# A sliding-window attention block inside a fused layer: 32 packed keys per query, values kept stationary in four column groups of TensorE, and the result regrouped by DMA

## The reference

```python
# attention block: 16 heads of 8, 4 key/value heads, window of 32 keys
h = layernorm(xn) ; q, k = rope(h @ Wq + bq), rope(h @ Wk + bk) ; v = h @ Wv + bv
valid = (col <= row) & (row - col < 32)
attn = softmax(where(valid, q @ k.T / sqrt(8), -1e9))
x1 = xn + (attn @ v) @ Wo + bo
y = x1 + gelu(layernorm2(x1) @ Wf1 + bf1) @ Wf2 + bf2      # hidden width 512
# experts: 8 of them, two per token; hidden width 448
z = sum over the token's two experts of g * (silu(xn @ w1.T) * (xn @ w3.T)) @ w2.T
```

## Time and profile before

| what | value |
|---|---|
| median of 3 runs | 540.97 us |
| profiled execution: its own time, its span | 541.51 us, 539.6 us |
| TensorE (PE) busy, share of the span | 461.3 us, 85% |
| VectorE (DVE) | 380.3 us, 70% |
| ScalarE (ACT) | 232.4 us, 43% |
| GpSimd (POOL) | 252.5 us, 47% |
| chain that ended last | PE 57%, DVE 22%, issue 11%, ACT 8% |
| largest lines of the chain | L1112 13%, L1074 11%, L1125 9%, L1053 6% |
| mean granted clock of TensorE | 0.913 of full speed |

### The profile page before, as it was taken

How to read it: one execution, slowest core, us unless ns; L and a number is a source line. 1 busy time by engine, 2 the same in 40 slices (tenths; PEclk the granted TensorE clock), 3 DMA queues, 4 the chain that set the end, 5 groups by cost and what they waited for, 6 DMA issues and landing times.

```text
span 539.6 us, 11287 instructions
## 1 busy us (share of the span) xinstructions
PE 461.3 (85%) x3102; PEld 408.8 (76%) x3103; DVE 380.3 (70%) x1132; ACT 232.4 (43%) x487; POOL 252.5 (47%) x373
## 2 busy tenths in 40 slices
PE   3921687898778999999999999999999998999967
PEld 2810476686668898888888998998988996675657
DVE  6868989779975847758578477584784753447784
ACT  2692433233251454445524544545335455454310
POOL 4626776744650734636437346363462425412520
PEclk9975777768777999999999999999999999999979
DMA  8961411100111455545544555454544540403042
GB/s 220 326 259 35 157 49 41 35 26 30 36 30 44 139 167 144 155 143 140 163 141 132 162 150 155 138 160 148 152 152 136 171 134 7 151 1 97 22 117 79
DMA packets 40571, 63.96 MB, mean 119 GB/s; under 512 B 6718, under 2 KB 27074, under 8 KB 40400
## 3 DMA queue, kind: packets, MB, share of 16 engines
q1 hardware_dynamic: 35456, 54.65, 33.3%
q0 software_dynamic: 4352, 8.47, 4.8%
q10 hardware_dynamic: 720, 0.30, 0.3%
HBM read 48.05 MB, written 15.87 MB: 118 GB/s over the span
## 4 chain that ended last, share of the span: by engine, by line
PE 57%; DVE 22%; issue 11%; ACT 8%; POOL 1%; DMA 1%; DVEq 0%; ACTq 0%; POOLq 0%
PE bank L1112 13%; PE bank L1074 11%; PE bank L1125 9%; PE bank L1053 6%; PE bank L1150 5%; PE bank L1139 4%; DVE rmax L650 3%; DVE pT L667 3%; DVE S L657 2%; PE bank L1086 2%; ACT L906 2%; DVE x_sb L740 2%; PE bank L1048 1%; DVE h L702 1%; ACT act L915 1%
## 5 line engine op out<-in xcount | busy, mean ns | idle before, releaser
L1112 PE MATMUL bank<-xsT,w_sb 128*128 128x128 f32 x1008 | 128.2, 279 | 4.4 <-DVE inter L730 2.7
L1112 PEld LDWEIGHTS bank<-xsT,w_sb 128*128 128x128 f32 x1008 | 119.5, 194 | 7.6 <-issue 5.4
L431 POOL DMA_INDIRECT scratch_ys<-ysb,pair x72 | 71.8, 997 | 36.1 <-issue 24.8
L1074 PEld LDWEIGHTS bank<-vbd,pT 128*128 128x128 f32 x512 | 73.7, 225 | 13.2 <-DVE pT L667 6.9
L1125 PE MATMUL bank<-w_sb,inter 128*128 x576 | 80.2, 282 | 4.1 <-issue 2.0
L1074 PE MATMUL bank<-vbd,pT 128*128 128x36 f32 x512 | 74.6, 303 | 10.3 <-DVE pT L667 9.2
L1125 PEld LDWEIGHTS bank<-w_sb,inter 128*128 128x128 f32 x576 | 71.8, 192 | 8.5 <-issue 7.0
L421 POOL DMA_INDIRECT scratch_xs<-xn_sb,slot x64 | 63.2, 988 | 31.5 <-issue 17.9
L243 POOL TENSOR_TENSOR spare_sb<-eps_sb 128x1 f32<-128x1 f32 x87 | 16.7, 192 | 128.0 <-ACT ysb L921 127.7
L1053 PE MATMUL bank<-kT,qbd 128*128 128x256 f32 x256 | 72.5, 410 | 0.0
L921 ACT ACTIVATE ysb<-bank 128x128 f32<-128x128 f32 x72 | 19.8, 275 | 114.8 <-PE bank L1125 114.8
(11 more groups left out here) (136 smaller groups left out, 692.9 us busy)
## 6 DMA issues: line engine op xcount, KB each, us to landing
w_sb<-in_w SPq DMA_DIRECT2D x72, 448.0 KB, 3.3
scratch_xs<-blank_sb SPq DMA_DIRECT2D x9, 520.0 KB, 6.0
xsb<-scratch_xs SPq DMA_DIRECT2D x72, 65.0 KB, 1.8
w_sb<-scratch_ys SPq DMA_DIRECT2D x8, 512.0 KB, 5.2
w_sb<-in_w SPq DMA_DIRECT2D x1, 2048.0 KB, 10.9
out_dram<-x_sb SPq DMA_DIRECT2D x8, 256.0 KB, 2.3
scratch_ys<-ysb,pair POOLq DMA_INDIRECT x72, 2.6
scratch_xs<-xn_sb,slot POOLq DMA_INDIRECT x64, 2.3
```

The source lines that it names most:

```text
L431: nc.gpsimd.indirect_dma_start(ys, bass.IndirectOffsetOnAxis(ap=pair[:, i % 3:i % 3 + 1], axis=0), ysb[:, i % 3, :], None, bounds_check=2 ...
L1074: last = nc.tensor.matmul(turn_bank[:, n * VW:(n + 1) * VW], pT[:, 2 * n + i].rearrange("p g q -> p (g q)"), vbd[:, p, n + i, :], start=(i ...
L1112: last = nc.tensor.matmul(to[:, c % EC * P:(c % EC + 1) * P], w13_sb[:, i % 3, c * P:(c + 1) * P], xsT[:, p, :], start=True, stop=True)
```

## The change

The diff, cut to its core. Loads and constants follow suit: `older_sb` is a 128 x 32 integer mask of "this place is taken by the older key", `newer_sb` is its complement, `neg_sb` a constant for the first block, which has no block before it; the sums' columns of the values are gone, `vmask_sb` (128 x 32) serves as the weights of the sums.

```diff
 # TensorE
-            def scores(b, p, u): ...          # mask product, two products of 256 columns; 4 calls a batch
+            def own_scores(b, p, h):
+                if some(2 * b + h):
+                    pe.wait_ge(own_kept, 2 * b + h)
+                for i in range(HALF):
+                    n = HALF * h + i
+                    last = nc.tensor.matmul(bank[0][:, i * GW:(i + 1) * GW], qbd[:, p, n].rearrange("p h q -> p (h q)"),
+                                            kT[:, p, :, (n + 1) * WIN:(n + 2) * WIN], start=True, stop=True)
+                last.then_inc(own_psum, 1)
+            def older_scores(b, p, h):
+                if some(2 * b + h):
+                    pe.wait_ge(chosen, 2 * b + h)
...
+                        last = nc.tensor.matmul(bank[1][:, i * GW:(i + 1) * GW], qbd[:, p, n].rearrange("p h q -> p (h q)"),
+                                                kT[:, p, :, n * WIN:(n + 1) * WIN], start=True, stop=True)
             def attend(b, p, quarter, h2T_out):
-                for n in range(quarter * NBLK // 4, (quarter + 1) * NBLK // 4):
-                    for i in range(2):
-                        last = nc.tensor.matmul(turn_bank[:, n * VW:(n + 1) * VW],
-                                                pT[:, 2 * n + i].rearrange("p g q -> p (g q)"),
-                                                vbd[:, p, n + i, :], start=(i == 0), stop=(i == 1))
+                a, total = quarter // 2, quarter % 2
+                for i in range(1 if total else 2):
+                    for c in range(4):
+                        n = 4 * a + c
+                        to = turn_bank[32 * c:32 * c + 32, total * T + a * P:total * T + (a + 1) * P]
+                        weights = (pO if i else pT)[:, n].rearrange("p g q -> p (g q)")
+                        values = vmask_sb if total else dv[:, p, n, :] if i else vbd[:, p, n, :]
+                        last = nc.tensor.matmul(to, values, weights, start=(i == 0), stop=(i == 1 or total == 1))
             def project(b, vt_out):
-                pe.wait_ge(outT_ready, b + 1)
+                pe.wait_ge(outT_in, 16 * 16 * (b + 1))
 # TensorE, step: scores(k, p, 0), (.., 1), (.., 2), (.., 3)  ->  own(.., 0), older(.., 0), own(.., 1), older(.., 1)
 # ScalarE
+            def keep_own(b, h):
+                act.wait_ge(own_psum, 2 * b + h + 1)
+                nc.scalar.activation(S[:, h], bank[0], ACT.Copy).then_inc(own_kept, 1)
 # VectorE
+            def shift(b, h):
+                dve.wait_ge(own_kept, 2 * b + h + 1)
+                wait_apart_dve("older_psum", older_psum, 2 * b + h + 1)
+                nc.vector.copy_predicated(half, bc(older_sb...), bank[1]...).then_inc(chosen, 1)
+                dve.wait_ge(chosen, 2 * b + h + 1)
+                nc.vector.tensor_reduce(rmax[:, h], half, AX.X, ALU.max).then_inc(rowmax_ready, 1)
+                dve.wait_ge(rowmax_ready, 2 * b + h + 1)
+                nc.vector.tensor_tensor(half, half, bc(rmax...), ALU.subtract).then_inc(shifted, 1)
             def norm(b):
-                nc.vector.reciprocal(rsum, pv[:, :, NKV * HD:VW]).then_inc(rsum_ready, 1)     # 128 x 32
+                nc.vector.reciprocal(rsum, turn_bank[:, T:2 * T]).then_inc(rsum_ready, 1)     # 128 x 256
-                nc.vector.transpose(outT, on).then_inc(outT_ready, 1)
+                nc.vector.tensor_tensor(on, turn_bank[:, 0:T], rsum, ALU.mult).then_inc(pv_normed, 1)
 # VectorE, step: the four shifts (2 x 128 x 256 each) and four transposes become two shifts (128 x 512) and two transposes,
 # both transposes at the start of the step
 # VectorE in steps 0 to 6, POOL from step 7 on: pO = pT where the key is of the own block, else 0 (128 x 1024)
+        def newer_part(ops, eng, b): ...
 # POOL: differences of neighbouring blocks of values (128 x 256)
+            def value_steps(b, p):
+                nc.gpsimd.tensor_tensor(dv[:, p], vbd[:, p, 1:NBLK + 1, :], vbd[:, p, 0:NBLK, :], ALU.subtract).then_inc(dv_ready, 1)
 # SyncE
+            def regroup(b):
+                sp.wait_ge(pv_normed, b + 1)
+                for c in range(4):
+                    src = on[c * 32:(c + 1) * 32, :].rearrange("c (a g q) -> c g a q", a=2, g=G)
+                    for g in range(G):
+                        dst = outT[g * 32:(g + 1) * 32, :].rearrange("c (a n q) -> c a n q", a=2, n=4)
+                        sp.dma_start(dst[:, :, c, :], src[:, g]).then_inc(outT_in, 16)
+            for b in range(LEAD - 1):
+                regroup(b)
             for g in range(GROUPS_A):
                 sp.wait_ge(scattered[g], 8 * 16)
             for p in range(3):
                 load_slots(0, p)
-            with sp.Fori(1, SLOT_TILES // 3) as n:
+            with sp.Fori(0, MSTEPS - 1) as m:
+                for n in range(1, 1 + TILES // 3):
+                    for p in range(3):
+                        load_slots(TILES // 3 * m + n, p)
+                        load_weights(TILES // 3 * m + n, p)
+                regroup(m + LEAD - 1)
...
+            regroup(B - 3)
+            regroup(B - 2)
...
             for i in range(4):
                 load_pairs(i)
+            regroup(B - 1)
```

More of the change, by code:

```diff
@@ L31 @@
 NBLK = T // WIN
-KW = 2 * WIN
-UNITS = NBLK // 2
-assert 2 * G * KW == 512 and UNITS == G
+HALF = NBLK // 2
+GW = G * WIN
+assert HALF * GW == 512
 DFF = 512
@@ L61, in layer @@
 def layer(nc, x, wqkv, bqkv, wo, bo, g1, b1, g2, b2, wf1, bf1, wf2, bf2, gate, w13, w2,
-          ident, cosf, sinf, maskadd, qmask, vmask, tri, rev, tilegrid, slotgrid, xs, ys, out):
+          ident, cosf, sinf, older, newer, qmask, vmask, tri, rev, tilegrid, slotgrid, xs, ys, out):
     F32, F32R, BF16, I32 = mybir.dt.float32, mybir.dt.float32r, mybir.dt.bfloat16, mybir.dt.int32
@@ L272, in rope_count, with in_lead, part_count, newer_part @@
             return (rope_ready_dve, b + 1) if early(b) else (rope_ready, b + 1 - EARLY)
+        def in_lead(b):
+            return isinstance(b, int) and b < LEAD - 1
+        def part_count(b):
+            return (pO_ready_dve, b + 1) if in_lead(b) else (pO_ready, b + 2 - LEAD)
+        def newer_part(ops, eng, b):
+            ready = pO_ready_dve if in_lead(b) else pO_ready
+            eng.wait_ge(pT_ready, 2 * b + 2)
+            if some(b):
+                eng.wait_ge(pv_psum, b)
+            ops.tensor_tensor(pO.rearrange("p n g q -> p (n g) q"), pT.rearrange("p n g q -> p (n g) q"),
+                              bc(newer_sb.rearrange("p (a q) -> p a q", a=1), [P, NBLK * G, WIN]), ALU.mult).then_inc(ready, 1)
         def add_bias(ops, eng, b):
@@ L334, in _ @@
                 load_weights(0, p)
-            for g in range(GROUPS_A):
-                sp.wait_ge(scattered[g], 8 * 16)
             def load_slots(n, p):
@@ L450, in step @@
                     tiles((-1,))
+                if exists(k - 1) and not in_lead(k - 1):
+                    newer_part(nc.gpsimd, pool, k - 1)
                 if group is not None:
@@ L458, in step @@
                 tiles((1,))
+                if exists(k):
+                    value_steps(k, p)
+                tiles((2,))
                 if exists(k + 2) and not early(k + 2):
@@ L461, in step @@
                     rotate(nc.gpsimd, pool, k + 2)
-                tiles((2, 3, 4, 5, 6, 7))
+                tiles((3, 4, 5, 6, 7))
                 if exists(k - 1):
@@ L471, in _ @@
             pool.wait_ge(bias_ready, 1)
+            pool.wait_ge(mask_in, 32)
             for k in range(LEAD):
-                step(k, group=k + 1)
-            step(LEAD, 0)
-            with pool.Fori(1, MSTEPS - 3) as m:
-                step(m + LEAD, m)
+                step(k, k % 2, group=k + 1)
+            step(LEAD, LEAD % 2, 0)
+            with pool.Fori(0, (MSTEPS - 4) // 2) as i:
+                step(2 * i + LEAD + 1, (LEAD + 1) % 2, 2 * i + 1)
+                step(2 * i + LEAD + 2, LEAD % 2, 2 * i + 2)
             for m in range(MSTEPS - 3, MSTEPS):
-                step(m + LEAD, m)
+                step(m + LEAD, (m + LEAD) % 2, m)
             scatter_y(MSTEPS, -1)
@@ L606, in _ @@
             dve.wait_ge(gate_in, 64)
-            nc.vector.tensor_copy(identb_sb, ident_sb)
-            for p in range(2):
-                last = nc.vector.tensor_copy(
-                    vbd[:, p, 1:NBLK + 1, NKV * HD:VW],
-                    bc(vmask_sb[:, NKV * HD:VW].rearrange("p (a c) -> p a c", a=1), [P, NBLK, NKV]))
-            last.then_inc(consts_set, 1)
+            nc.vector.tensor_copy(identb_sb, ident_sb).then_inc(consts_set, 1)
             dve.wait_ge(bias_ready, 1)
```

171 lines of the change are left out of this document (82 added, 89 removed).

## The result

The changed kernel takes 632.23 us (median of 4 runs, 623.9 to 634.38). The kernel before takes 540.71 us beside it (539.51 to 542.07). The ratio is 1.163 (1.152 to 1.173): slower by 91 us where 27 were forecast, and outside the range.

A forecast was written before the change was run, and what follows sets the result against it. TensorE was taken to bound the loop, busy 34.17 of 36.35 us a step. Lead 0, junction +11, loop gain -18, loop stalls +20 and tail +14 gave +27 on 540.97, so 568 us, range 546 to 600.

The forecast's parts named there:

- The price of an issue: SyncE's queue: 0.47 us per regrouping DMA, issue to issue, 7.5 us a batch; low end 0.38, high 0.62.
- Junction: Before the first tile: the lead's last regrouping stands ahead of the first slot loads, nothing else can run; +11 us.
- The loop's stall: In the loop, seven times: slots and weights come late behind the regrouping, 2.9 us each, +20; ends 1.4 and 5.3.
- The clock rival: Rival: TensorE's clock falls to the low level after each of seven stalls, +1.8 x 7, total 583 us; chance 0.08.
- POOL ... hides them at no cost: GpSimd in the loop: its spare time covers the newer part's 2.6 us; without that cover 3.3 us a step.
- The loop's gain: Loop: 0.9 us of TensorE's time and 1.4 of gaps saved, 2.3 us x 8 steps, -18 us; bounds 0.3 and 4.3.
- The column groups: Attention times values on TensorE: 5.3 us in turn, 1.3 with four at once; middle 3.3 taken, no change.
- The lead: Attention rounds ahead of the first tile: 16.2 us each, no change, regrouping hidden behind attention; bounds -7 and +20.
- The tail: Kernel's end: pair loads wait behind batch 14's regrouping, last projection behind batch 15's; +15, less 1 counted before, +14 us.
- quick queue: Rival: SyncE issues at 0.38 us and four column groups run at once; -10 us, total 530; chance 0.16.
- no overlap: Rival: TensorE's column groups run in turn, +2 us x 8 in the loop, 2.5 x 6 in the lead, 599; chance 0.14.
- The change doesn't do what it says: Rival: half-width softmax brings nothing, VectorE being covered by TensorE; loop gives 0.9 a step, 579 us; inside the forecast's range.

The follow-up runs named there:

- before_dmas: Kernel before, with the same 16 DMAs a batch added at the same places of SyncE's queue, into an unread buffer: 612.17 us, ratio 1.134.
- one_dma: Changed kernel with one DMA in place of a batch's 16, the regrouping itself left out: 553.75 us, ratio 1.025.
- newer_dve: Changed kernel with the newer part made by VectorE in all steps, not by GpSimd from the loop on: 633.3 us, ratio 1.172.
- all_spread: Changed kernel, regrouping DMAs spread over next step's loads, GpSimd's rotation split between stores, ScalarE's first score copy behind tile 1's silu: 583.29 us, ratio 1.028.
- all_spread_dve2: The same kernel as all_spread_dve, run again on another chip: 543.07 us, ratio 1.001 to the kernel before.
- all_spread_dve: all_spread with the newer part made by VectorE throughout: 563.12 us, ratio 0.989 to the kernel before.
- last_split: all_spread_dve with half of the last batch's regrouping DMAs issued by ScalarE's queue: 558.65 us, ratio 0.980 to the kernel before.

## Why the prediction was wrong in size

- **Direction and places: right.** Sixteen issues between `norm` and the next loads cost time at the junction, in each loop step and in the tail, and outweigh the gain. before_dmas shows this alone.
- **The price of an issue** ("I take 0.47: 7.5 us a batch"): mis-sized. It is 0.64 from start to start, 10.2 to 10.9 us a batch. The end of the forecast's range, 0.62, was the better choice. Its 0.15 for the third dimension had no row behind it; the rows of 0.43 were of DMAs with two dimensions, and the single DMA of one_dma, SBUF to SBUF with two, takes 0.46, but no run changes the number of dimensions alone. *Junction*: up products at 178.66 for 165.92, 15.5 us after the reciprocal instead of 1.5, +14.0 for +11; 2.7 of the missing 3 are the issues'.
- **The loop's stall** ("The delay is 2.9 us, 7 x 2.9 = +20"): the step that failed. Its own figures give 3.1 (252.9 less 249.8), and 5.3 with the right price, by its own upper end. By one_dma the queue with all that follows from it costs 6.2 us a step, 43 us in seven, and the rows of the seven steps divide it: 3.8 are longer gaps (8.2 for 4.4; the stops for slots alone are 3.7 a step), 2.3 are TensorE's busy time, 35.2 for 32.8 with the same products, at a granted clock of 0.93 for 0.99. So the stop was put 0.9 too low, and the clock behind it was put at nothing. The clock rival, with 0.08, came true besides: it was priced as one group of up products (1.8), and as an alternative to the forecast, not as a term that comes with the stop. The forecast's own upper price of an issue and its clock rival, put together, would have given about 607 us, an estimate, already outside the range.
- **"POOL ... hides them at no cost": wrong**, and in a way that the forecast had no term for. GpSimd's busy share allowed the 2.36 us. But VectorE's small operation stands still beside it, which rows of the kernel before show on a smaller scale (0.83 for 0.21). VectorE's waits for the stores (L765, 11.5 us, 0.6 before) have another cause: they stay in newer_dve and go in all_spread. What the operation costs was covered by the queue in the changed kernel as it is (newer_dve); without the queue it is 1.2 to 2.5 us a step.
- **"The loop's gain ... 2.3 us"**: too high. TensorE's own saving was underestimated: attention times values was put at no change, and with the scores TensorE's busy time fell by 1.4 us a step at the same clock (33.8 to 32.4 in all_spread_dve2, over the seven steps), not by 0.9. But the gaps, of which 1.4 were to close, grew by 0.5 (1.7 to 2.2). So a step gains 0.9 us in the best order. In the kernel as it was run the loop's miss of 7.3 us a step is thus 3.3 for the stall with its clock, 1.2 for GpSimd's operation, 1.4 for the orders and 1.4 for the gain that was not there.
- **The column groups**: between its two ends (5.3 and 1.3) the middle was taken. By the chain a pair of quarters now takes 0.57 and 0.35 us, 1.8 a batch with both pairs: near the end of full overlap.
- **The lead** ("I put the 16.2 us at no change"): right as a sum, -1.2 us for all of it. Its reason was wrong in part: the projection there waits for the regrouping, which one_dma shows to be worth 9 us of the lead. That the relief of the engines hides it is argued: no run takes the relief away alone.
- **The tail** (+14): +14.2 over its three rows. The issues cost more (the last projection 13.6 us after the reciprocal for a forecast of 11.7), and about 2 us came back in the work after it.
- **The rivals**: quick queue and no overlap are out, each by its own row. "The change doesn't do what it says" was close for the softmax: VectorE has 25.09 us of work in the step before and after, since L765's 2.8 us more (5.44 for 2.66) took what the rest of the change gave (22.3 without them, near the relief of 2.9 that was forecast).

What stays open: why all_spread_dve gains 1.1% on a chip of one kind and nothing on one of the other, with the same loop step on both. It is the kernel before that differs more: it loses 27 us on the slower kind, this one 20, all of them ahead of its first reciprocal. There is no trace of the kernel before from such a chip that would show where its other 7 go. last_split was run only there, so that it beats the kernel before is shown for that kind alone; on the other it was not run.

## What to carry to other kernels

A transposition by 16 small DMAs costs little in bytes and much in the queue: count issues times their start-to-start spacing, and ask who stands behind them, since in the loop the same 16 cost nothing once they were dealt out over the tiles. A stop of an engine is not only its own length: price the slower clock behind it in the sum. When two delays lie side by side, taking off the shorter shows nothing; take off the longer first, and then test the other again, as the same edit went from nothing to 3.5% here.

## What the hardware showed that was not expected

- VectorE's operation on 128 x 1 took 2.78 us instead of 0.21 while GpSimd multiplied 128 x 1024. The Trainium skill has the rule ("SBUF — State Buffer", Who interferes with whom): a VectorE instruction with two inputs in SBUF contends with a GpSimd instruction that reads SBUF, over ports that it calls an exclusive lock. The trace agrees: L765 reads `xsb` and `slotgrid_sb`, and in seven steps it stands for 2.48 to 2.78 us and ends 0.02 to 0.03 us after GpSimd's row. Its own row begins ahead of GpSimd's each time, so the rows don't show why it is VectorE that waits. The products of `gated`, one input of which is in PSUM, were not slowed (L773 has 0.56 us throughout).
- Four column groups of f32 products run at once: 0.43 us for eight records against 1.06 in one group.
- A DMA from SBUF to SBUF of 32 partitions x 2 x 128 bytes takes 0.60 us to issue on SyncE and 0.62 on ScalarE; small loads of two dimensions took 0.43, one DMA of 128 x 1 KB from SBUF to SBUF 0.46, the loads of slots in the loop 0.34.
- A reciprocal from PSUM takes 1.746 us for 256 columns; with 0.350 for 32 that is 6.2 ns a column, as two rows of before had foretold.
